# High and low halves in one 128-row pass for the attention scores of a single-core MetaFormer kernel

## The reference

```
q, k, v = x @ wqkv + bias                       # 12 heads, 16 channels each
scores  = (q * 16**-0.5) @ k.T
scores += q . rel_h[h_q - h_k] + q . rel_w[w_q - w_k]
probs   = softmax(scores)
x       = x + (probs @ v) @ wproj + bproj
```

## Time and profile before

| what | us |
|---|---|
| median of 3 runs | 499.08 (497.39 to 500.5) |
| profiled execution, whole | 498.38 |
| profiled execution, span from first to last instruction | 496.5 |
| TensorE busy | 460.4 (93%) |
| VectorE busy | 344.9 (69%) |
| ScalarE busy | 235.0 (47%) |
| GpSimd busy | 172.6 (35%) |
| mean granted TensorE clock | 0.993 of full speed |

### The profile page before, as it was taken

How to read it: one execution, slowest core, us unless ns; L and a number is a source line. 1 busy time by engine, 2 the same in 40 slices (tenths; PEclk the granted TensorE clock), 3 DMA queues, 4 the chain that set the end, 5 groups by cost and what they waited for, 6 DMA issues and landing times.

```text
span 496.5 us, 8916 instructions
## 1 busy us (share of the span) xinstructions
PE 460.4 (93%) x3064; PEld 379.6 (76%) x3064; DVE 344.9 (69%) x780; ACT 235.0 (47%) x594; POOL 172.6 (35%) x171
## 2 busy tenths in 40 slices
PE   6999899998979899999889898899989999989997
PEld 5855699998645599999555565555679999979997
DVE  3665698997565598998476467441189899878764
ACT  1366365552257394643167147322237655537442
POOL 6044436643026345563025305210046566300000
PEclk9899999999999999999999999999999999989999
DMA  5650055540390044650279500602214565435551
GB/s 150 237 141 1 1 176 172 181 140 1 120 300 1 0 162 137 212 159 2 74 191 307 159 0 1 191 2 109 114 62 137 199 204 176 152 88 171 177 183 34
DMA packets 19347, 62.36 MB, mean 126 GB/s; under 512 B 4025, under 2 KB 6898, under 8 KB 19314
## 3 DMA queue, kind: packets, MB, share of 16 engines
q1 hardware_dynamic: 19314, 61.93, 38.9%
HBM read 59.82 MB, written 2.10 MB: 125 GB/s over the span
## 4 chain that ended last, share of the span: by engine, by line
PE 70%; issue 11%; DVE 9%; POOL 4%; DMA 4%; ACT 2%; SPq 1%; POOLq 0%; DVEq 0%
PE bank L953 25%; PE bank L965 10%; PE bank L977 8%; PE bank L768 6%; PE bank L979 4%; PE bank L794 3%; PE bank L807 3%; POOL probs L424 2%; DMA rel<-rel_scratch 2%; POOL rstd L391 2%; PE bank L663 1%; DVE nmax L1155 1%; PE bank L751 1%; PE bank L696 1%; PE bank L655 1%
## 5 line engine op out<-in xcount | busy, mean ns | idle before, releaser
L953 PE MATMUL bank<-xT_hi,w_hi 128*128 128x256 f32 x408 | 109.6, 290 | 1.2 <-issue 1.2
L1195 DVE TENSOR_TENSOR w_lo<-w,w_hi 128x512 fp32r<-128x512 f32 x102 | 96.9, 988 | 2.1
L602 ACT ACTIVATE hid<-bank,b 128x256 f32<-128x256 f32 x150 | 62.7, 471 | 68.7 <-PE bank L953 68.5
L953 PE MATMUL bank<-xT_hi,w_lo 128*128 128x256 f32 x408 | 82.0, 282 | 0.0
L953 PEld LDWEIGHTS bank<-xT_hi,w_hi 128*128 128x128 f32 x408 | 78.1, 191 | 3.4 <-issue 3.3
L444 POOL TENSOR_TENSOR w_hl<-w,consts 128x384 fp32r<-128x384 f32 x50 | 52.5, 1049 | 73.4 <-PE bank L979 69.7
L424 POOL TENSOR_TENSOR probs<-probs,rinv 128x512 f32<-128x512 f32 (+1 forms) x44 | 42.8, 991 | 99.0 <-DVE rinv L1159 99.0
L953 PEld LDWEIGHTS bank<-xT_hi,w_lo 128*128 128x128 f32 x408 | 63.5, 191 | 0.0
L977 PE MATMUL bank<-w_hl,hid_hi 128*128 128x384 f32 x200 | 61.6, 373 | 0.0
L446 POOL TENSOR_TENSOR w_hl<-w,w_hl 128x384 fp32r<-128x384 f32 x50 | 58.9, 1178 | 3.9
L965 PE MATMUL bank<-w,hid 128*128 128x192 f32 x308 | 56.4, 327 | 2.3 <-issue 2.3
(11 more groups left out here) (159 smaller groups left out, 662.3 us busy)
## 6 DMA issues: line engine op xcount, KB each, us to landing
w<-in_M_w_dram SPq DMA_DIRECT2D x34, 768.0 KB, 5.4
w<-in_M_w_dram SPq DMA_DIRECT2D x33, 576.0 KB, 3.8
w<-in_M_w_dram SPq DMA_DIRECT2D x9, 288.0 KB, 2.8
wqkv<-in_A_wqkv_dram SPq DMA_DIRECT2D x4, 432.0 KB, 6.9
rel_scratch<-relall SPq DMA_DIRECT2D x4, 372.0 KB, 2.3
wproj<-in_A_wproj_dram SPq DMA_DIRECT2D x4, 288.0 KB, 7.8
wqkv<-in_M_w_dram SPq DMA_DIRECT2D x2, 576.0 KB, 18.0
kT<-in_M_w_dram SPq DMA_DIRECT2D x2, 576.0 KB, 6.5
```

Source lines behind the costliest of these rows:

```text
L602: ins = act.activation(hid[:, 2 * b + c, :], bank[B_H[b]][:, c * T:(c + 1) * T], FUNC[cfg["act"]], bias=b1[:, kb, bass.ds(at, 1)])
L953: ins = pe.matmul(bank[B_H[b]][:, c2 * T:(c2 + 1) * T], w, xs, start=(q == 0), stop=(q == 4))
L1195: dve.tensor_tensor(w1_cols(w1_lo, b), w1_cols(w1[s], b), w1_cols(w1_hi, b).bitcast(F32), ALU.subtract)\
```

## The change

Scores are computed from halves. For each head, 64 rows hold k as high, low, high and zeros, and q as high, high, low and zeros, so that one float32r pass sums high x high, high x low and low x high. The other 64 rows of the 128 hold the high and low halves of the relative terms (in q) against one-hot rows (in k). Each head has its own matmul of 128 rows and 256 columns, and `qT` is twice as large. To get there:

- VectorE writes full k and q (`kf`, `qf`, part of `att_out`), ScalarE writes their high halves twice into the staging tiles, VectorE subtracts to get the low halves.
- Relative terms are split by ScalarE and VectorE in the same way, laid into `q_st` over the transposed q, and transposed in a second round of 12 transposes, with evictions of their own.
- The one-hot rows of `kT` are transposed once at the start and copied by ScalarE over all pairs (`onehot_rows`), in attention 0 and once more before attention 1. GpSimd stages them and clears less at the start; before attention 3 it clears the whole of `qT`.
- In attention 0 the rows from the small matmuls are split too.
- The load of the constants goes ahead of the loads of attention 0. Several tiles now share memory; the weights of experts 6 and 7 of experts block 2 go to other places and wait also for the last projection.

Cut to its core:

```diff
-                    act.wait_ge(pool_ready, 4)
+                    act.wait_ge(pool_ready, 2)
+                for t in range(TT):
+                    act.wait_ge(f_ready, 2 * (TT * n + t) + 1)
+                    act.activation(high_low(k_st, t)[:, :, 0:3:2], kf[:, t].rearrange("p (n d) -> p n d", n=NH).unsqueeze(2)
+                                   .broadcast_to([P, NH, 2, HD]), ACT.Copy).then_inc(k_hi_ready, 1)
+                    act.wait_ge(f_ready, 2 * (TT * n + t) + 2)
+                    act.activation(high_low(q_st, t)[:, :, 0:2], qf[:, t].rearrange("p (n d) -> p n d", n=NH).unsqueeze(2)
+                                   .broadcast_to([P, NH, 2, HD]), ACT.Copy).then_inc(q_hi_ready, 1)
...
+                if ATTN[n]["rel"]:
+                    for t in range(TT):
+                        act.wait_ge(rel_in[t], 16 * sum(sides(i) for i in range(n + 1)))
+                        act.activation(rel_slots(t, 0, 2 - sides(n)), rel_values(t, 2 - sides(n)), ACT.Copy).then_inc(rel_hi_ready, 1)
+                    for b in range(3):
+                        act.wait_ge(qr_psum, 3 * n + b + 1)
+                        act.activation(qT[0:SLOT, 2 * b:2 * b + 2, 1, :],
+                                       bank[B_KT[b]][0:SLOT, :].rearrange("p (a t) -> p a t", a=2), ACT.Copy).then_inc(qr_act, 1)
...
+            def onehot_rows(src):
+
+                for head in range(2):
+                    row = rel_row(head)
+                    act.activation(kT[row:row + SLOT, :, head, :], src[row:row + SLOT, :].unsqueeze(1).broadcast_to([SLOT, PAIRS, T]),
+                                   ACT.Copy).then_inc(hotT_ready, 1)
...
-                    for t in range(TT):
-                        pe.matmul(scores_bank(n, p, t), qT[:, p, t * P:(t + 1) * P], kT[:, p, :, 0:keys_of(n, t)],
-                                  start=True, stop=True).then_inc(s_psum, 1)
+                    if p < 2 and ATTN[n]["rel"]:
+                        pe.wait_ge(qr_act, 3 * n + p + 1)
+                        pe.wait_ge(qr_dve, 3 * n + p + 1)
+
+                    for t in range(TT):
+                        for h in range(2):
+                            ins = pe.matmul(scores_bank(n, p, t)[:, h], qT[:, p, h, t * P:(t + 1) * P], kT[:, p, h, 0:keys_of(n, t)],
+                                            start=True, stop=True)
+                        ins.then_inc(s_psum, 1)
...
+                    dve.wait_ge(f_ready, 2 * (TT * n + t) + 2)
+                    dve.wait_ge(k_hi_ready, TT * n + t + 1)
+                    dve.tensor_tensor(high_low(k_st, t)[:, :, 1], kf[:, t].rearrange(heads, h=NH),
+                                      high_low(k_st, t)[:, :, 0].bitcast(F32), ALU.subtract).then_inc(k_ready, 1)
+                    dve.wait_ge(q_hi_ready, TT * n + t + 1)
+                    dve.tensor_tensor(high_low(q_st, t)[:, :, 2], qf[:, t].rearrange(heads, h=NH),
+                                      high_low(q_st, t)[:, :, 0].bitcast(F32), ALU.subtract).then_inc(q_ready, 1)
...
-            pool.memset(kT[:, :, :, :], 0.0).then_inc(pool_ready, 1)
...
+                        pool.memset(qT[:, :, :, :].bitcast(F32), 0.0).then_inc(q_clear, 1)
```

More of the change, by code:

```diff
@@ L268, in sides, with kw_rows, rel_row, high_low @@
             return 1 if n == 0 else 2
-        def rel_copies(n, t):
-            return sum(TT * sides(i) for i in range(n)) + (t + 1) * sides(n)
         def kw_bank(i, row):
             return bank[B_REL[i]][row:row + SIDE, 0:3 * P].rearrange("p (a k) -> p a k", a=3)
-        def kw_rows(i, head):
-            row = head * SLOT + HD + SIDE
+        def kw_rows(i, head, row):
             return kT[row:row + SIDE, 3 * (i // 2):3 * (i // 2) + 3, head, (i % 2) * P:(i % 2 + 1) * P]
+        def rel_row(head):
+            return SLOT * (1 - head)
+        def high_low(tile, t):
+            return tile[:, t].rearrange("p n (g s) -> p n g s", s=HD)
+        def rel_slots(t, part, first):
+            return q_st[:, t].rearrange("p (a h) s -> p a h s", h=2)[:, :, ::-1, part * 32 + first * SIDE:part * 32 + 2 * SIDE]
+        def rel_values(t, first):
+            return rel[:, t, first:2].rearrange("p a r n -> p (a r) n").rearrange("p s (a h) -> p a h s", h=2)
         block = ctx.enter_context(nc.Block())
@@ L1080, in attn @@
                     dve.wait_ge(aw_in[n], 96 if n else 80)
[L1081 removed]
+                    then(dve.tensor_scalar(bq4[:, :], bqkv[:, n, 0:C], scale, None, ALU.mult))
                     for h in range(KC):
@@ L1128, in attn @@
-                    dve.tensor_copy(kw_rows(i, 1), kw_bank(i, SLOT + HD + SIDE)).then_inc(kw_dve, 1)
-                rows = HD + SIDE if n == 0 else SLOT
+                    for head in range(2):
+                        row = rel_row(head)
+                        dve.wait_ge(kw_act, 2 * i + head + 1)
+                        dve.tensor_tensor(kw_rows(i, head, row + 32), kw_bank(i, row), kw_rows(i, head, row).bitcast(F32), ALU.subtract)\
+                            .then_inc(kw_dve, 1)
                 for b in range(3):
@@ L1139, in attn @@
+                if n == 3:
+                    dve.wait_ge(q_clear, 1)
+                for b in range(3):
+                    dve.wait_ge(qT_psum, 3 * n + b + 1)
+                    dve.tensor_copy(qT[SLOT:P, 2 * b:2 * b + 2, 1, :],
+                                    bank[B_QT[b]][SLOT:P, :].rearrange("p (a t) -> p a t", a=2)).then_inc(qT_dve, 1)
                 if ATTN[n]["rel"]:
```

202 lines of the change are left out of this document (119 added, 83 removed).

## The result

The changed kernel takes 507.67 us (median of 4 runs, 507.14 to 511.96); the kernel before, run beside it, 499.38. The ratio is 1.0195 (95% interval 1.0152 to 1.0238): clearly slower, and about 2%; whether it is more or less than 2% stays open. The profiled execution takes 507.17 us with a span of 505.4, against 498.38 and 496.5. The forecast of 501.5 had the sign and missed the size: +8.9 us of span where the sum said +3.1. That the time lies at the 507.5 of rival A is chance; that mechanism turns out to be less than half of the excess (2.9 of the 6.2 us by which the four stages exceed the sum).

The account below looks back on a forecast made before the run. TensorE was taken to bound the pairs, with a ScalarE and VectorE loop next; 9.1 us won there against preparation losses of 5.7, 1.9, 3.1 and 1.5 gave +3.1, 501.5 us, range 495 to 508.

Parts of the forecast that it names:

- the sum: All attention stages: -9.1 + 5.7 + 1.9 + 3.1 + 1.5 = +3.1 us on the profiled 498.38, giving 501.5.
- rival A: Half clock: TensorE's waits drop its clock to 0.50 at the start of attentions 0 to 2, +6 to 507.5; chance 0.17.
- The pairs: Six head pairs, attentions 0 to 2: first maximum to last scaling 17.8 us for 20.8, 9.1 us won in all.
- the second loop: Exponentials on ScalarE, then reciprocal and next maximum on VectorE: 2.77 us a pair, the bound once TensorE needs 2.34.
- Preparation, attentions 1 and 2: Work before the first maximum: VectorE's longer queue, alternating with ScalarE, loses 1.9 us in attention 1, 3.1 in attention 2.
- Attention 0: Preparation there: one-hot copies, split key rows and evictions put the first maximum at 32.7 against 27.03, 5.7 us lost.
- the other end, 7.2: Attention 0's loss if VectorE's 1.78 us first scaling came from its place, not from GpSimd's clearing beside it.
- rival A's bracket: Attention 0: the earlier start at 11.05 may spare the first clock fall, half of 2.71 us, 1.3 won.
- Attention 3: No gain counted in its pairs; alternation and six VectorE evictions delay the mask add, 1.5 us lost.
- B: Preparation overlaps: half of the 12.2 us lost is hidden behind early ScalarE work, 495.4, or 493 with more; chance 0.17.
- C: No single pass: the new score matmuls cost 0.48 us each, the 9.1 isn't won, 510.6; chance 0.04.
- D: Dearer copies: ScalarE's strided 384-column copies 0.60 apart, not 0.38, 504, or 506.3 if VectorE waits on all; chance 0.14.

Follow-up runs that it names:

- three-matmul warming: Changed kernel plus warming matmuls: 3 before keys' transposes, 4 more before relative terms' transposes, 3 more before first transposes of probabilities (attentions 0 to 2); 505.62 us.

## Why the prediction was right or wrong

Of the 6.2 us by which the four stages exceed the sum, 2.85 lie in the pairs, 2.5 in the tails and 0.85 in the preparations.

**The pairs: right at a steady clock, 2.7 us short without it.** The sum had 17.8 us from first maximum to last scaling. With the clock held it is 17.75 or 17.76 in attentions 0 and 1 and 17.94 to 17.96 in attention 2, in four different kernels, so the count of the second loop was good to 0.2. (The 0.2 more of attention 2 is the end of ScalarE's table load, which puts its first exponentials 0.93 instead of 0.73 us behind the maximum.) The changed kernel has 18.20, 18.90, 19.08. The step that failed is "the second loop becomes the bound" as the only consequence of a lighter TensorE: at the half clock eight transposes take 1.91 us instead of 1.04, and TensorE is the bound for 6 us again. This is rival A's mechanism, to which 0.17 was given, at half its size: 2.9 us by the three-matmul warming, not 6, and it varies, since the same three attentions took 2.8 us more in another run. Its point of decision was wrong too. I had it decide where a wait outlasts 2.08 us. That fits attention 0 (3.02 us ahead of the fall at 25), but in attention 1 the waits ahead of the fall are 1.83 and 1.95, and the kernel before idles 2.24 us ahead of its q transposes in attention 1 and stays at 1.00. What sets the fall is left open.

**The end of the attention: not in the sum, +2.5 us.** I followed the pairs to the last scaling and let the rest move with it: this term was put at nothing without a reason. TensorE's queue behind that point holds transposes, sums over values and two projections of 0.75 us each. With pairs 3.8 us apart, it had caught up when the last scaling ended; with pairs 2.8 apart it hasn't. The changed kernel with full scores (6.58) and the kernel before with the pass alone (7.40) show that it comes with the pass, and moving both projections behind took 0.85 away. Which share is the projection's and which the transposes' wait for VectorE's copy was not separated.

**Preparation, attentions 1 and 2: +2.67 and +3.88 for 1.9 and 3.1.** Each step down to the projection bias started within 0.15 us of its forecast. The failed step is the price of the copies that read relative terms: I took all 384-column instructions by their number, 0.38 apart, and named 0.60 as the other end. For the copies into slots at L536 and L539 the near end was good (0.43 apart); for those that read in another order, ScalarE pays about 0.8 apiece, past both ends. On the path it was only 0.30 of the 0.77 missing. Of the other 0.47, 0.23 stood already ahead of the low relative terms (they start at 143.14, less 3.41 that is 139.73 for 139.5); the rest is spread over handovers, and no run assigns it.

**Attention 0: +5.14 for 5.7,** too long by 0.56. The scaling took 0.26 as forecast, and putting GpSimd's clearing back, which made it 2.02, shows why; the other end, 7.2, is out. It also waited for the wproj load until 9.93, forecast 9.8; relative matmuls began at 11.12 for 11.05 and took 1.50 us instead of 2.71, at the full clock: the 1.3 won that rival A's bracket names. At the end of VectorE's evictions of q about 1.0 of it was left (27.94 for 28.9), and 0.5 at the first maximum, 32.19 for 32.7: from there to the end of the low relative terms it took 1.46 for 1.0.

**Attention 3: +1.35 for 1.5,** right, and it wins nothing from the pass: right. Half of the loss, 0.70, goes with the split; the rest stays with the evictions that remain. The clearing of qT and the later expert loads cost nothing: right, expert block 2 takes 41.02 us for 41.04.

**Rivals.** B, overlap: wrong, the preparations lost 13.0 us and not half of 12.2. C: wrong, 0.145 a pass. D: wrong in its place; it priced all copies at the far end, and only the reading ones were dear.

## What to carry to other kernels

When a bound is taken away, follow the chain past the point where it ended before, to the stage's own end: work queued on the relieved engine (here two projections and the last sums) is late there, and moving one of them gained 3.1 us in the kernel before as well. A gain that makes TensorE idle may have to pay for its clock: count the idle stretches, fill each with no more matmuls than it holds, and judge by pieces of the stage, since the clock falls of the same instructions differed by 2.8 us between executions. Price a copy by the order in which it reads, not by its columns alone.

## What the runs showed of the hardware

- TensorE's granted clock fell to 0.50 after idle stretches of 1.83 and 1.95 us in attention 1, and stayed at 1.00 after a single one of 2.24 us in the kernel before. Four kernels with three more warming matmuls ahead of the first transposes of probabilities had 1.00 in the pairs of attentions 0 to 2.
- Where it falls changes from run to run: attention 1's preparation had it at 139 to 142 with that filling and at 140 to 143 in a run without, and attention 3's had it, at a cost of 1.34 us, in two kernels with more filling and in one with none. Why isn't settled.
- VectorE's scaling that met GpSimd's clearing ended with the last of two clearings back to back (11.85 and 11.74), though the first ended at 11.06: 2.02 us instead of 0.26.
- ScalarE and VectorE took 0.88 and 0.83 us apiece for 384 fp32 columns read 48 bytes apart, 0.53 and 0.55 for the same read in order.
